# The third pair of expert outputs leaves the vector engine: copied with its gate weights by ScalarE, added by GpSimd

## The reference

```python
def _L0_ffn_ref(x, in_proj_w, ..., gate_w, gate_b, expert_w, expert_b, ln1_w, ...):
    # H = 16 heads, D = 16, NE = 8 experts, TOP_K = 2
    xh = x.reshape(B, S, H, D)
    q_in = k_in = _apply_rope(xh, sin, cos).reshape(B, S, E)
    ...
    attn = softmax(where(causal, q @ k.T / sqrt(D), -inf)); ctx = attn @ v
    attn_out = ctx @ out_proj_w.T + out_proj_b
    x1 = _layer_norm(x + attn_out, ln1_w, ln1_b)
    gates = softmax(x1 @ gate_w.T + gate_b)
    _, top_idx = top_k(gates, 2)
    top_gates = take_along_axis(gates, top_idx)
    expert_outputs = einsum('bsd,efd->bsef', x1, expert_w) + expert_b
    sel = take_along_axis(expert_outputs, top_idx[..., None], axis=2)
    moe_out = sum(sel * top_gates[..., None], axis=2)
    return _layer_norm(x1 + moe_out, ln2_w, ln2_b)
```

## Time and profile before

| | |
|---|---|
| median of 3 executions | 1463.17 us (1463.01 to 1466.61) |
| the profiled execution | 1462.98 us, span 1461.2 us |
| PE busy | 1404.3 us, 96% |
| DVE busy | 1101.8 us, 75% |
| ACT busy | 785.1 us, 54% |
| POOL busy | 428.2 us, 29% |
| PE idle, waiting for the DMA `qs<-nmT` | 13.7 us in 14 waits |
| last matmul ends | 1450.47 us after the span's start |

### The profile page before, as it was taken

How to read it: one execution, slowest core, us unless ns; L and a number is a source line. 1 busy time by engine, 2 the same in 40 slices (tenths; PEclk the granted TensorE clock), 3 DMA queues, 4 the chain that set the end, 5 groups by cost and what they waited for, 6 DMA issues and landing times.

```text
span 1461.2 us, 28046 instructions
## 1 busy us (share of the span) xinstructions
PE 1404.3 (96%) x9600; PEld 762.2 (52%) x9600; DVE 1101.8 (75%) x2736; ACT 785.1 (54%) x1707; POOL 428.2 (29%) x707
## 2 busy tenths in 40 slices
PE   8889999999999999999999999999999999999996
PEld 6767655555445445354556555555533344555442
DVE  3765878888788887787547887788877787878657
ACT  3235365455655565665665355554565556666651
POOL 4434423322232222121434443323211110110234
PEclk9999999999999999999999999999998999999999
DMA  3865422230221131110125232213020101111100
GB/s 111 207 165 131 119 60 56 56 85 25 59 57 49 35 78 40 40 42 20 49 65 120 79 89 67 56 53 81 20 52 20 25 21 26 32 24 32 38 26 15
DMA packets 150843, 88.61 MB, mean 61 GB/s; under 512 B 113854, under 2 KB 143862, under 8 KB 150447
## 3 DMA queue, kind: packets, MB, share of 16 engines
q1 hardware_dynamic: 150703, 86.83, 23.6%
HBM read 60.71 MB, written 25.43 MB: 59 GB/s over the span
## 4 chain that ended last, share of the span: by engine, by line
PE 74%; DVE 8%; issue 4%; ACT 3%; SPq 2%; DMA 1%; POOL 1%; POOLq 0%; DVEq 0%; ACTq 0%
PE bank L1389 17%; PE bank L1367 14%; PE bank L1502 14%; PE bank L1339 13%; DVE mxs L1034 3%; PE bank L1459 2%; ACT pbuf L947 2%; PE bank L1437 2%; SPq L775 1%; PE bank L1445 1%; PE bank L1343 1%; PE bank L1372 1%; DMA qs<-nmT 1%; PE bank L1420 1%; PE bank L1478 1%
## 5 line engine op out<-in xcount | busy, mean ns | idle before, releaser
L1034 DVE TENSOR_REDUCE mxs<-bank 128x1 f32<-128x512 f32 (+3 forms) x1120 | 713.8, 667 | 172.1 <-PE bank L1339 98.2
L947 ACT ACTIVATE pbuf<-bank 128x512 f32<-128x512 f32 (+1 forms) x1112 | 592.9, 595 | 382.1 <-PE bank L1389 207.7
L1367 PE MATMUL bank<-qs,ks 99*128 99x256 bf16 (+3 forms) x1536 | 426.6, 321 | 17.0 <-DMA qs<-nmT 13.7
L1339 PE MATMUL bank<-ks,qs 96*128 96x512 bf16 (+3 forms) x1280 | 424.4, 351 | 4.7 <-ACT pA L979 1.1
L1389 PE MATMUL bank<-pbuf,vcur 128*17 128x256 f32 (+3 forms) x3072 | 272.8, 473 | 2.4 <-ACT pbuf L947 2.3
L1367 PEld LDWEIGHTS bank<-qs,ks 99*128 99x128 bf16 x1536 | 140.1, 98 | 201.4 <-issue 95.2
L1502 PE MATMUL bank<-ew,x1T 128*128 128x512 f32 x464 | 221.9, 600 | 0.3 <-DVE acc L1268 0.3
L1339 PEld LDWEIGHTS bank<-ks,qs 96*128 96x128 bf16 x1280 | 123.8, 99 | 137.6 <-issue 52.7
L1389 PEld LDWEIGHTS bank<-pbuf,vcur 128*17 128x17 f32 x3072 | 70.6, 97 | 144.0 <-issue 98.0
L1502 PEld LDWEIGHTS bank<-ew,x1T 128*128 128x128 f32 x464 | 82.1, 190 | 69.7 <-issue 60.5
L892 POOL TENSOR_TENSOR accp<-etmp 128x256 f32<-128x256 f32 x29 | 21.0, 724 | 244.1 <-ACT etmp L927 244.1
(11 more groups left out here) (278 smaller groups left out, 1748.6 us busy)
## 6 DMA issues: line engine op xcount, KB each, us to landing
vcur<-v_scratch SPq DMA_DIRECT2D x92, 136.0 KB, 2.4
parts_scratch<-parts SPq DMA_DIRECT2D x29, 384.0 KB, 3.3
xw<-windows SPq DMA_DIRECT2D x29, 256.0 KB, 2.9
qs<-parts_scratch SPq DMA_DIRECT2D x32, 192.0 KB, 3.3
ks<-parts_scratch SPq DMA_DIRECT2D x32, 192.0 KB, 3.6
ks<-parts_scratch SPq DMA_DIRECT2D x32, 128.0 KB, 2.7
qs<-parts_scratch SPq DMA_DIRECT2D x32, 128.0 KB, 3.6
v_scratch<-vst SPq DMA_DIRECT2D x29, 136.0 KB, 1.8
```

Source lines behind the costliest of these rows:

```text
L947: nc.scalar.activation(pbuf[:, u0:u0 + heads, nj * P - cols:nj * P], bk[:, 0:heads * cols].rearrange("p (h t) -> p h t", h=heads), ACT.Exp)\
L1034: v.reduce_max(mxs[:, j * HJ + h:j * HJ + h + heads, c], bk[:, 0:heads * cols].rearrange("p (h t) -> p h t", h=heads), AX_X)\
L1339: last = mm(bk[:, x * cols:(x + 1) * cols].rearrange("p (n t) -> p n t", t=P), qs5[0:KR, pos % QRING, j, head, :], ks5[0:KR, kslot, 0:cols ...
L1367: last = mm(bk[:, x * cols:(x + 1) * cols].rearrange("p (n t) -> p n t", t=P), ks5[0:KR + NPART, kslot, kb % GT, head, :], qs5[0:KR + NPAR ...
```

## The change

Pair 2 is treated as pairs 1 and 3 are. ACT copies both experts with their weights into `etmp` once pair 1 has been added, POOL adds both halves to `accp` in two dependent adds, and pair 3 waits for that instead of for pair 1. The semaphore `e2_half` goes, `accp_half` and `accp3_ready` come. `g_y` no longer waits for pair 2 on DVE. The table of steps gets the new engine, durations and waits, and with them the planned order changes.

```diff
-        add("f_e2c", T, "DVE", 860, ("f_e2", T), ("f_e0c", T))
+        add("f_e2c", T, "ACT", 750, ("f_e2", T), ("f_e1a", T))
+        add("f_e2a", T, "POOL", 1400, ("f_e2c", T), ("f_e1a", T))
         add("f_e3", T, "PE", 1720, ("f_e2", T))
-        add("f_e3c", T, "ACT", 750, ("f_e3", T), ("f_e1a", T))
-        add("f_e3a", T, "POOL", 700, ("f_e3c", T), ("f_e1a", T))
+        add("f_e3c", T, "ACT", 750, ("f_e3", T), ("f_e2a", T))
+        add("f_e3a", T, "POOL", 700, ("f_e3c", T), ("f_e2a", T))
...
+                elif name == "f_e2a":
+                    pool.wait_ge(*drain("f_e2", T))
+                    pool.wait_ge(accp1_ready, T + 1)
+                    pool.tensor_tensor(accp[f], accp[f], etmp[f][:, 0, :], ALU.add).then_inc(accp_half, 1)
+                    pool.wait_ge(accp_half, T + 1)
+                    pool.tensor_tensor(accp[f], accp[f], etmp[f][:, 1, :], ALU.add).then_inc(accp3_ready, 1)
                 elif name == "f_e3a":
                     pool.wait_ge(*drain("f_e3", T))
-                    pool.wait_ge(accp1_ready, T + 1)
+                    pool.wait_ge(accp3_ready, T + 1)
...
-                elif name in ("f_e1c", "f_e3c"):
+                elif name in ("f_e1c", "f_e2c", "f_e3c"):
                     k = int(name[3])
                     act.wait_ge(*fill(name[:4], T))
-                    if name == "f_e3c":
+                    if name == "f_e2c":
                         act.wait_ge(accp1_ready, T + 1)
+                    elif name == "f_e3c":
+                        act.wait_ge(accp3_ready, T + 1)
...
-                elif name in ("f_e0c", "f_e2c"):
-                    k = int(name[3])
-                    half = e0_half if k == 0 else e2_half
+                elif name == "f_e0c":
+                    k, half = 0, e0_half
                     dve.wait_ge(*fill(name[:4], T))
-                    dve.wait_ge(*drain("f_b" if k == 0 else "f_e0", T))
+                    dve.wait_ge(*drain("f_b", T))
...
                 elif name == "g_y":
                     dve.wait_ge(esum_ready, T + 1)
-                    dve.wait_ge(*drain("f_e2", T))
+                    dve.wait_ge(*drain("f_e0", T))
```

More of the change, by code:

```diff
@@ L300, in stage_steps @@
         add("g_xb", T, "POOL", 700, ("g_load", T), ("load_b2", 0))
-        add("g_y", T, "DVE", 330, ("f_es", T), ("f_e2c", T))
+        add("g_y", T, "DVE", 330, ("f_es", T), ("f_e0c", T))
         add("g_st", T, "DVE", 330, ("g_y", T))
@@ L641, in build @@
                              "w_ready", "wts_ready"))
-        e0_half, e2_half = sem("e0_half"), sem("e2_half")
+        e0_half, accp_half, accp3_ready = sem("e0_half"), sem("accp_half"), sem("accp3_ready")
         accp1_ready, accp2_ready, esum_ready = sem("accp1_ready"), sem("accp2_ready"), sem("esum_ready")
```

## The result

| | before | after |
|---|---|---|
| median | 1465.64 us (6 runs, 1463.01 to 1466.61) | 1471.12 us (6 runs, 1469.96 to 1475.15) |
| ratio | | 1.0045, 95% interval 1.0029 to 1.0062 |
| profiled execution, span | 1462.98, 1461.2 | 1469.96, 1468.0 |
| last matmul ends | 1450.5 | 1455.8 |
| from there to the end of the span | 10.7 | 12.2 |

The changed kernel is slower by 5.5 us at the median, 0.45%. The forecast was plus 4.0 (0.27%), 1467 us with a range of its own from 1464 to 1471. The median of 1471.12 lies just above that range: the change cost 1.5 us more than forecast, and the kernel before, over six executions and not three, stands at 1465.64 and not at 1463.17. Measured again beside other kernels, 12 runs against 35 of the kernel before, the ratio was 1.0034 (1.0018 to 1.0051).

A forecast was written before the change was run, and what follows sets the result against it. PE, busy 96% of the span, was taken as the bound, DVE at 75% not. Terms 0 + 0.5 + 2.1 + 1.4 + 0 gave plus 4.0 us, forecast 1467 us, own range 1464 to 1471, 8 in 10 from 1458 to 1474.

The forecast's parts named there:

- Middle, 0: Middle tiles: removed DVE sums and added copies and adds lie under PE's matmuls; 0 us, bounds minus 2 to plus 2.
- margin of 0.9 us on pair 3: Middle tile: pair 2's adds end near 448.8, pair 3 on PE at 449.7, so its new wait is met 0.9 us early.
- Ends of jobs, plus 0.5: PE's waits for the maxima's DMA at job ends: job 19 plus 0.4, job 30 at most 0.1; bounds minus 1 to plus 2.
- job 30's queue on SP: Job 30's store now goes ahead of the maxima, but its last norm is issued earlier on DVE: at most plus 0.1 us.
- The end, plus 2.1: From last o_T to last matmul: 26.0 us against 23.9, less work to hide the chain under; bounds plus 0.9 to 4.1.
- the 1.9 us of small steps: Small steps said to move ahead of the last o_T with five pairs (8.6 us), making o_T 10.5 us later.
- the sign that I had named: The forecast would be wrong if PE idled less after o_T than the 4.7 us of before.
- Slow clock, plus 1.4 (0 to 2.1): PE idle 2.3 us before tile 30's row transpose brings 1.2 GHz: 3.8 us more, 1.8 hidden in the wait for weights.
- After the last matmul, 0 (0 to plus 1): Last tile: pair 3's copy waits about 0.9 us for pair 2's adds, overlapping a POOL norm step that already delayed the add.
- DVE and POOL on one memory: New POOL adds meeting DVE's two-input norm steps cost up to 0.5 us each; 0.4 to 0.8 in the end, inside the bounds.
- faster: Rival, 17%: DVE bounds some stretches, waits at jobs 30 and 31 shrink and the clock holds; minus 5 to minus 9 us.
- Slower by more: Rival, 18%: pair 3's copy, waiting for POOL's adds, blocks ACT with exponentials queued behind it; 1472 to 1478 us.

The follow-up runs named there:

- e1_old_order: The changed kernel's instructions in the order planned for the kernel before, the two new steps where pair 2's sums stood; 1473.71 us, 1.0058 to before.
- e10_warm: The changed kernel plus useless matmuls: 12 ahead of job 30's first st, 8 ahead of job 31's, 8 ahead of tile 30's row transpose; 1466.99 us, 1.0010 to before.
- e5_tail_dve: The changed kernel in its own order, but pair 2 of tiles 28 to 31 summed by DVE as before; 1468.76 us, 1.0018 to before.
- e2_new_order: The kernel before's instructions (pair 2 summed by DVE) in the order planned for the changed kernel; 1469.62 us, 1.0027 to before.
- e11_before_both: The kernel before with job 30's maxima transpose ahead of tile 21's f_e0 and 7 useless matmuls ahead of job 31's first st; 1461.72 us, 0.9977.
- e9_swap30: The kernel before with the transpose of job 30's maxima moved ahead of tile 21's expert pair f_e0 on PE; 1462.89 us, 0.9978 to before.
- e7_before_cover: The kernel before, its order planned with 1.75 us more between the maxima's write and the first st from job 8 on; 1467.17 us, 1.0014.

## Why the prediction was right in sign and where its terms failed

- **Middle, 0.** Right, at plus 0.3 and 0.6. Jobs 9 to 29 lose 12.6 us before and 12.9 and 13.2 after. But the margin of 0.9 us on pair 3 was read from one tile, in the old order, and does not hold for all. In e1_old_order, where pair 3 was not moved back, ten copies wait 0.7 to 1.3 us for the adds, and the price in jobs 9 to 29 is 3.7 us. What kept it near 0 is the planner's shift of pair 3, which the forecast named only in passing.
- **Ends of jobs, plus 0.5.** Measured plus 0.7 and 0.8 in jobs 30 and 31, inside the bounds. The waits for the maxima in jobs 9 to 29 grew by 0.8 and 1.1 us besides. The step that was short is job 30's queue on SP, which I priced at 0.1. The wait went from 2.76 to 3.17, the 0.41 that the store takes to be issued:

```profile
1104.91 0.41 SPq L797 DMA_DIRECT2D out<-x0f  x1
1105.37 2.95 SPq L776 DMA_DIRECT2D qs<-nmT  x4
1109.52 0.50 PE L1375 MATMUL bank<-qs,ks 99*128 99x512 bf16 x1 [3.17 <-DMA qs<-nmT]
```

Between job 32 and `o_T` another 0.9 us of small waits came, for which I had no term.
- **The end, plus 2.1.** The chain was right and the base wrong. From `o_T` to the last matmul I forecast 26.0 us without the clock; measured 30.2 - 4.6 = 25.6, and 28.7 - 3.0 = 25.7 in the repeat. e10_warm, where the clock is 1.00 throughout, takes 26.1. But the same end of before I put at 34.4 - 10.5 = 23.9. The work behind `o_T`, without losses, was 34.4 - 4.7 = 29.7 and is 30.2 - 4.5 - 4.6 = 21.1. It shrank by 8.6, the five pairs, and not by 10.5: the 1.9 us of small steps is the term that failed. What moved with the five pairs is two biases and one weight transpose, under 0.3 us by the distances between their starts. So before's end lies at 25.8 and the chain costs nothing more. That the 26.0 came out is luck: it held 19.2 us of work and 6.8 of idle time, and there were 21.1 and 4.5. Idle after `o_T` is 4.5 us, against 4.7: by the sign that I had named, this term is wrong.
- **Slow clock, plus 1.4 (0 to 2.1).** The mechanism was right: idle 2.06 us, forecast 2.3, then 0.50. The size was not: 4.6 and 3.0 us. I had let 1.8 us hide in a wait for the weights of tile 30, and that wait does not exist. With the clock at 1.00, in e10_warm, it is 0.23 us, because the weights come 5.8 us after the gate and not 6.8:

```profile
1441.24 0.22 PE L1506 MATMUL bank<-idb,wpad 128*128 128x128 bf16 x1 [0.23 <-DVE wpad L1254]
```

So nearly all of what the slow pairs and gates took longer counted in full. The term's own sum does not come out either: 3.8 less 1.8 is 2.0, and plus 1.4 was written.
- **After the last matmul, 0 (0 to plus 1).** Failed: plus 1.5, in both profiles of the changed kernel, gone in e5_tail_dve. I let pair 2's adds overlap with a norm's step of the other tile. Both are on POOL and queue, as above.
- **DVE and POOL on one memory.** The forecast's 0.4 to 0.5 us a meeting is seen once more. In the end of the changed kernel the same sum takes 0.93 us beside a POOL add and 0.42 seven microseconds later without one:

```profile
1453.77 0.93 DVE L1281 TENSOR_TENSOR ks<-ks,parts 128x256 f32<-128x256 f32 x1 [1.56 <-POOL parts L906]
1460.76 0.42 DVE L1281 TENSOR_TENSOR ks<-ks,rxT 128x256 f32<-128x256 f32 x1 [0.68 <-POOL rxT L906]
```

The first runs beside the add that POOL starts at 1453.69. It is what the Trainium skill's page "SBUF — State Buffer", section "Who interferes with whom", leads one to expect. Middle losses grew by 0.3 and 0.6 us only, so the new adds met nothing there that counts.

The terms as measured, in the first profile: 0.3 + 0.7 + 0.9 - 0.2 + 4.6 + 1.5 = plus 7.8, and 0.6 + 0.8 + 1.0 - 0.1 + 3.0 + 1.5 = plus 6.8 in the repeat. The medians say plus 5.5 and 5.9. What is missing is the slow clock at jobs 30 and 31, 6.7 us in the one profile of before and 3.3 and 4.4 in the two of after. How much of that belongs to the kernels is open: the old order showed 6.7, 4.7 and 6.5, the new one 3.3, 4.4, 3.3, 6.1 and 4.4.

That plus 4.0 came as near to plus 5.5 as it did is luck in part. Of its terms 2.1 us (the chain) did not come. Against them stand 1.6 to 3.2 more for the slow clock, 1.5 after the last matmul and 0.9 ahead of `o_T` without a term.

Two readings of the rows in the prediction were off. The clock in the kernel before fell three times ahead of the last matmul, not twice. The third is at 85.6 us, where a wait of 2.33 us for the maxima (at 89.3) is the second longest of the 14; there the clock was at 0.50 before that wait began. And four of the six idle times after `o_T` are in rows 8, not three.

Of the rivals, *faster* was wrong: no kernel with the lighter DVE was measured faster than the kernel before. *Slower by more* named the right mechanism, ACT held by POOL with exponentials behind, and it decides in the old order and in the last tile. The planner had moved it out of the way elsewhere.

## What to carry to other kernels

A copy into a buffer that another engine must empty first makes every instruction behind it on that queue wait too; before work is moved to such a chain, find where the copy stands and what queues behind it, in the last tile above all. Here, with the tensor engine 96% busy, relief of an engine at 75% was worth nothing that could be measured, while one transpose moved ahead of one pair of experts, so that a wait of 2.8 us became 1.2 and the clock held, was worth 0.22%. When steps are moved ahead of a mark, count them one by one from the two orders before the rest is called shorter.

## What the runs showed of the hardware that I had not expected

- The slow clock differs in length behind the same wait. Before tile 30's row transpose PE was idle for 2.06, 2.06, 2.11 and 2.06 us in after, its repeat, e2_new_order and e5_tail_dve; it then ran at 1.2 GHz for about 10, 7, 3.4 and 3.4 us.
- The waits that matter can be shorter than I took. In before and e11_before_both an idle of 1.33 us after `o_T` was followed by no slow clock, and in e9_swap30 the same idle of 1.33 by 3.4 us of it. It followed an idle of 1.26 us in e1_old_order, and idles of 0.68 and 0.46 us, starting a microsecond apart, in e7_before_cover. In the kernel before the clock fell at 85.6 us with no idle of PE over 0.6 us in the 5 us ahead of it.
- The first 194 us, with the same order on PE, lost from 19.0 to 24.2 us. PE's wait for the input tiles (`xw<-windows`) alone was 1.6 us in before and 2.1 to 4.2 in the others with that order.
